# A graph network on one core: in the message passes, the edge-feature matmuls of the next octet move behind the scatter matmuls of the present one

## The reference

```
for l in range(5):
    h_in = h + vn[batch]
    emsg = relu(h_in[src] + edge_attr @ We[l] + be[l])
    agg  = segment_sum(emsg, dst, num_segments=4096)
    t    = h_in + agg
    t    = relu(t @ W1[l] + b1[l]) @ W2[l] + b2[l]
    ...                       # batch norm, relu, residual, virtual node
```

## Time and profile before

| | |
|---|---|
| median of 3 runs | 9051.75 us (9049.84 to 9053.43) |
| the profiled execution, its own time | 9054.67 us |
| its span in the trace | 9052.8 us |
| PE busy over the span | 6297.6 us (70%) |
| POOL busy | 5940.7 us (66%) |
| DVE busy | 4270.4 us (47%) |
| mean granted TensorE clock | 0.841 |

### The profile page before, as it was taken

The page is one execution under the profiler, slowest core; times in us unless marked ns, Lnnn a source line. Parts: engine busy times, 40 slices in busy tenths (PEclk is TensorE's granted clock), DMA queues, the critical chain, the costliest instruction groups (busy, mean ns, idle before and its releaser), DMA issues. The chain is left out here.

```text
span 9052.8 us, 128356 instructions
## 1 busy us (share of the span) xinstructions
PE 6297.6 (70%) x27247; PEld 4650.6 (51%) x27248; DVE 4270.4 (47%) x9200; ACT 1899.1 (21%) x5238; POOL 5940.7 (66%) x5947
## 2 busy tenths in 40 slices
PE   3678767967786786777777335667856776776775
PEld 2456645745674575566345334545644454454444
DVE  6555555455545555554223734456673234224224
ACT  3332332323233333323443100011110000000000
POOL 2776477467737756772775477757756775775776
PEclk9899889989998998898789755569877898888788
DMA  5443344244424424442332000023313332332332
GB/s 166 125 128 104 97 128 127 66 135 127 123 78 129 127 83 121 127 125 70 101 103 79 17 8 3 3 74 100 94 43 97 102 102 89 102 100 83 102 103 86
DMA packets 424175, 855.05 MB, mean 94 GB/s; under 512 B 142497, under 2 KB 206754, under 8 KB 424098
## 3 DMA queue, kind: packets, MB, share of 16 engines
q0 software_dynamic: 263184, 679.84, 26.3%
q1 hardware_dynamic: 160914, 174.39, 6.5%
HBM read 790.64 MB, written 63.18 MB: 94 GB/s over the span
## 5 line engine op out<-in xcount | busy, mean ns | idle before, releaser
L262 POOL DMA_INDIRECT ring<-node_table,idx x4608 | 4535.8, 984 | 1739.4 <-issue 1679.6
L332 PE MATMUL psAT<-ring,S 128*128 128x256 f32 x13680 | 3924.6, 439 | 1104.7 <-DVE AGG L376 513.2
L332 PEld LDWEIGHTS psAT<-ring,S 128*128 128x128 f32 x13680 | 2808.3, 216 | 2192.7 <-issue 937.4
L235 DVE SCALAR_TENSOR_TENSOR S<-iota,block_start,dst_f 128x512 f32<-128x512 f32 x1900 | 1422.0, 748 | 1603.0 <-PE psAT L332 1512.1
L350 ACT ACTIVATE ring<-ring 128x256 f32<-128x256 f32 x2560 | 958.5, 416 | 2218.8 <-DVE ring L391 2214.0
L391 DVE TENSOR_TENSOR ring<-ring,psE 128x256 f32<-128x256 f32 x2560 | 964.2, 417 | 810.8 <-DMA ring<-node_table,idx 715.0
L376 DVE TENSOR_TENSOR AGG<-AGG,psAT 128x256 f32 x864 | 361.7, 419 | 1057.8 <-PE psAT L332 1057.8
L301 PE MATMUL psE<-we_stk,stk 128*128 128x256 bf16 x2560 | 396.8, 283 | 543.6 <-DVE ring L391 457.4
L246 ACT COPY idx<-src_i 128x8 int32 x704 | 138.7, 197 | 2675.9 <-DMA ring<-node_table,idx 1974.4
L262 POOL DMA_INDIRECT ring<-att_table,idx x512 | 527.0, 1029 | 249.4 <-issue 221.4
L431 POOL DMA_INDIRECT gs<-score_table,idx x512 | 521.3, 1018 | 163.8 <-issue 155.7
(11 more groups left out here) (268 smaller groups left out, 4271.4 us busy)
## 6 DMA issues: line engine op xcount, KB each, us to landing
stk<-stack_table SPq DMA_DIRECT2D x320, 256.0 KB, 2.8
ring<-node_table,idx POOLq DMA_INDIRECT x4608, 2.8
node_table<-tab SPq DMA_DIRECT2D x224, 128.0 KB, 1.7
stack_table<-stk SPq DMA_DIRECT2D x64, 256.0 KB, 2.0
gs<-score_table,idx POOLq DMA_INDIRECT x512, 2.4
ring<-att_table,idx POOLq DMA_INDIRECT x512, 2.8
w_sb<-in_L_gnn_W SPq DMA_DIRECT2D x10, 512.0 KB, 9.8
att_table<-tab SPq DMA_DIRECT2D x32, 132.0 KB, 1.8
```

The source lines that it names most:

```text
L235: nc.vector.scalar_tensor_tensor(S[:, 4 * g:4 * g + 4, :], iota[:, :].unsqueeze(1).to_broadcast([P, 4, P]), block_start[:, bass.ds(blk, 1) ...
L262: nc.gpsimd.indirect_dma_start(ring[:, q, 0:gw], None, table, bass.IndirectOffsetOnAxis(ap=idx[:, q:q + 1], axis=0)).then_inc(gathered[q], 16)
L332: ins = nc.tensor.matmul(psA[:, 0:D], S[:, u, :], ring[:, q, 0:D], start=(u == 0), stop=(u == U - 1))
```

## The change

The block that calls `encode` for the next octet moves from ahead of the octet's units to behind them, and behind the `octet_free` that follows them. The last octet of each round gets one more semaphore increment, on `idx_seen`, which no instruction waits for. `encode(0, 0)` ahead of the loop stays.

```diff
@@ -307,13 +307,6 @@
                     with pe.Fori(0, NG) as i:
                         for ob in range(OB):
                             h = OB * i + ob
-                            if kind == MESSAGE:
-
-                                if ob < OB - 1:
-                                    encode(i, ob + 1)
-                                else:
-                                    with pe.If(i < NG - 1):
-                                        encode(i + 1, 0)
                             cnt = pe.value_load(span_row[0:1, bass.ds(2 * h + 1, 1)], min_val=1, max_val=NB)
 
                             def unit(_, first):
@@ -337,6 +330,14 @@
 
                             units(pe, None, cnt, unit)
                             pe.drain().then_inc(octet_free, 1)
+                            if kind == MESSAGE:
+
+                                if ob < OB - 1:
+                                    encode(i, ob + 1)
+                                else:
+                                    with pe.If(i < NG - 1):
+                                        encode(i + 1, 0)
+                                    pe.sem_inc(idx_seen, 1)
```

## The result

The changed kernel takes **10,138.28 us** (median of 4 runs, 10,131.13 to 10,140.0) against 9,052.59 us for the kernel before (4 runs). The ratio is 1.1197, with a 95% interval of 1.1178 to 1.1217. The forecast was slower, 10,325, in a range of 10,040 to 10,610.

The account below looks back on a forecast made before the run. Gathers on POOL set the pace; the change makes a serial chain of 897.4 us a message pass for 640.5. Four passes at +256.9 and one at +246.0 give +1273.6, so 10,325 us, range 10,040 to 10,610.

Parts of the forecast that it names:

- The bound before: In the message passes POOL's gathers set the pace, 10.3 us an octet; a pass took 640.5 us.
- The chain: Per octet, scatter, encode, additions, one-hots and next scatter run without overlap; 11.9 us for an octet of one unit.
- The links: Times of the chain's pieces, read where the trace shows them bare; summed to 897.4 us a message pass.
- last encode to the first addition: 0.37 us: Gap between PE's last encode and DVE's first addition, 0.37 us, counted 63 times a pass.
- first unit: 6.0 us: Scatter of each octet's first unit on PE, taken as 6.0 us; bounds 3.72 and 6.83.
- scatter to encode: 0.45 us: Gap on PE from scatter end to first encode, taken as 0.45 us between readings of 0.26 and 0.61.
- The clock: PE stands still 4.41 us ahead of each scatter, so first units begin at low clock: 6.0 us, not 3.72.
- the mean granted clock: PE's granted clock over the message pass falls from 0.86 and 0.94 in its halves to some 0.7.
- The full clock (9,597): Rival: the chain forms but PE's clock stays up, first units 3.72 us; +544 us, 9,597; chance 6%.
- The low clock throughout (10,865): Rival: everything behind PE's wait runs low, first units 6.83 and encodes 1.91 us; +1813, 10,865; chance 4%.
- No change: Rival: POOL's 10.3 us pace and the ring's four slots hide the chain; 9,052; chance 1%.
- faster: Rival: scatters start sooner, so POOL's waits for PE go, at most 60 us; 8,992; chance 2%.

Follow-up runs that it names:

- e11: The kernel before with two additions of no use and a drain on DVE behind each octet's eight additions: 9,054.55 us, ratio 1.0002.
- e10: The changed kernel with two additions of no use and a drain on DVE behind each octet's eight additions: 10,606.09 us, ratio 1.172 to the kernel before.
- e6: The changed kernel with 16 matmuls of no use (512 columns) behind each encode inside the loop: 11,823.87 us, ratio 1.0703 to the kernel before, on a slower chip.
- e8: The changed kernel with four of the next octet's eight encodes moved back ahead of the scatter: 11,221.65 us, ratio 1.0169 to the kernel before, on a slower chip.
- e7: The changed kernel with DVE's one-hots and sums ahead of its message additions: 11,156.41 us, ratio 1.0118 to the kernel before, on a slower chip.
- e12: The kernel before, PE's order kept, with DVE's one-hots and sums ahead of its message additions: 9,964.94 us, ratio 1.1012.
- e5: The changed kernel again, unchanged, on a slower chip: 11,390.54 us, ratio 1.0327 to the kernel before.

## Why the prediction was right, and where its sizes were off

- **The bound before** was right. The gathers set the pace; e11 shows that DVE did not, 1.1 us more on it in each octet for a ratio of 1.0002. That the other passes would keep their time was right too, to about 1 us in 668 for the last PLAIN pass.
- **The chain** was right, in its stages and their order. The timeline of 1295 to 1315 us above shows each link, and e10 shows that its length sets the time: 1.1 us more in each octet came out in full, and more.
- **The links.** Encodes 1.04 and second units 4.43 us were as taken. Three terms of the sum were too large; 1273.6 us were forecast and 1083.1 came:
  - *last encode to the first addition: 0.37 us* was 0.04 (1301.20 + 1.04 to 1302.28): 63 x 0.33 x 5 = 104 us. This is the largest error. The row it was taken from, 1062.69 in the earlier trace rows, had its one-hots end at 1062.33 only, and DVE's own sequencer was at work from 1061.74 to 1062.64, with the load of the octet's span (L215, 0.31 us) among it. So the 0.37 us were time that DVE needed to get to its next addition and not a delay of the semaphore. In the changed kernel DVE has long done this when the encodes end.
  - *first unit: 6.0 us* was (487.9 - 31 x 3.72)/64 = 5.82: 58 us.
  - *scatter to encode: 0.45 us* was, from 24.3 us in all, about 0.38: 21 us.

  Together 183 of the 190.5 us. The first of them is a misreading of a row; the forecast stayed in its range in spite of it.
- **The clock** was right in kind. The scatters' busy time grew from 395.1 to 487.9 us a pass, 464 us in five, 43% of the growth. That is an account of where the time went, and not what a full clock would give back: with all first units at 3.72 us the 320 of them would take 5 x 64 x 2.10 = 672 us less, an estimate from the means above, as some ran low in the kernel before as well (14 of the second pass begin at 0.50). e10 (longer wait, slower scatters) and e6 (no wait, 63 of 64 first units fast) show that the wait makes it. Wrong was the forecast of the mean granted clock, some 0.7, for 0.80 and 0.82 in the halves of the pass; the prediction gives no working for it. By the Trainium skill, "TensorE: Matmul & The Clock Gate", section "HAM oscillation — how this bites in real kernels", each burst behind a wait starts cold. The trace agrees for 49 of the 64 first units, that of 1306.30 among them, and not for the 15 that begin at 1.00; nor does the low level last: the window behind the scatter of 1306.30 stands at 1.00, and the mean first unit takes 5.82 us, between 3.72 at 1.00 and the 6.68 of this one.
- **The rivals.** The full clock (9,597) failed on the first units of 5.82 us. The low clock throughout (10,865) failed on encodes of 1.04. No change and faster failed on the time itself and on POOL's 214.7 us of waits for PE. On the slower chip e8 and e7 give back 45% and 63% of the loss without touching the encodes' number, as the chain would have it.

## What to carry to other kernels

Where two engines hand one buffer back and forth, what lets them overlap is that one of them is a step ahead; moving that step behind the work it used to run under makes a chain of everything between, and its price is the sum of the links, not the length of the moved step (1.04 us moved here, 3.4 us an octet lost). Check both engines' orders together: here a new order on PE alone cost 12% and one on DVE alone (e12) 10%, while both at once (e7) cost 1.2% on a chip where PE's alone cost 3.3%. When a link is priced from a timeline row, look at what its engine was doing until then; a wait that ends late may be the engine's own. And tell the kinds of a group apart before taking its mean: in e6 the scatters' total hid first units that had become fast and second units that had become slow.

## What the runs showed of the hardware that was not expected

On two chips every version took longer, the kernel before 11,016.73 and 11,218.57 us for 9,052.59. The changed kernel moved the same 424175 packets and 855.05 MB there (e5) as on the chip of the result. The stall stands in PLAIN passes too: in e5 the gathers' starts in the last one span 10488.3 to 11272.6, 784.2 us for 668.8 on the chip of the result. A timeline of e5 in the PLAIN pass before that:

```profile
9891.91 3.72 PE L325 MATMUL psAT<-ring,S 128*128 128x256 f32 x16 [1.22 <-issue]
...
9903.58 0.95 POOL L262 DMA_INDIRECT ring<-node_table,idx  x1 [0.30 <-issue]
9906.71 0.20 ACT L246 COPY idx<-src_i 128x8 int32 x1 [9.97 <-DMA ring<-node_table,idx]
9907.50 0.42 DVE L377 TENSOR_TENSOR AGG<-AGG,psAT 128x256 f32 x1 [10.44 <-remote]
```

The scatter ended at 9895.63 (9891.91 + 3.72). DVE built one half of the one-hots at 9896.31 and then stood for 10.44 us, up to the sums of 9907.50, while POOL issued gathers without a pause up to 9904.5. The additions of e5 above have 73.9 us a pass of idle time with that releaser (remote), those of the changed kernel on the chip of the result none. What causes them stays open: no run was made for it, and no trace of the kernel before was taken on these chips.
